# Graph network, two layers on one core: the products with the count matrix as whole float32 products, degrees in two halves, moments of x1 by accumulators

## What is computed

```python
h = relu(layernorm(x))
# layer 0
msg = (h[src] + edge) @ Wm.T + bm
agg = segment_sum(msg, dst) / max(deg, 1)
u   = concat(h, agg) @ Wu.T + bu
o   = layernorm(h + gelu(u)) * gamma + beta
x1  = x + o
# layer 1
h1    = relu(layernorm(x1))
neigh = segment_sum(h1[src], dst)
y     = relu(((1 + eps) * h1 + neigh) @ W1 + b1) @ W2 + b2
out   = x1 + y + h1
```

## Time and profile before

| | us |
|---|---|
| median of 3 runs | 487.54 (486.55 to 487.87) |
| the profiled execution | 488.46 |
| span of the profiled execution | 486.7 |
| TensorE busy (matmul) | 471.4 |
| VectorE busy | 266.0 |
| ScalarE busy | 165.5 |
| GpSimd busy | 120.6 |

### The profile page before, as it was taken

The page is one execution under the profiler, slowest core; times in us unless marked ns, Lnnn a source line. Parts: engine busy times, 40 slices in busy tenths (PEclk is TensorE's granted clock), DMA queues, the critical chain, the costliest instruction groups (busy, mean ns, idle before and its releaser), DMA issues.

```text
span 486.7 us, 9356 instructions
## 1 busy us (share of the span) xinstructions
PE 471.4 (97%) x3297; PEld 281.4 (58%) x3297; DVE 266.0 (55%) x614; ACT 165.5 (34%) x312; POOL 120.6 (25%) x185
## 2 busy tenths in 40 slices
PE   7999999999999999999999999899999999999997
PEld 5545545455545456777766655799744449444442
DVE  4798886778787878876958699923000000011011
ACT  6677642333333338412047287620012213000000
POOL 4016343443344331000001113249980000000000
PEclk9999999999999999989999999999999999999999
DMA  8999999999999999996330111040230000010111
GB/s 283 382 396 408 408 386 373 403 392 406 401 373 393 407 404 398 369 349 237 147 105 23 43 43 40 5 170 1 56 118 0 0 0 1 22 43 23 43 43 38
DMA packets 31720, 98.92 MB, mean 203 GB/s; under 512 B 3672, under 2 KB 4696, under 8 KB 31674
## 3 DMA queue, kind: packets, MB, share of 16 engines
q1 hardware_dynamic: 30458, 97.27, 52.9%
q10 hardware_dynamic: 1216, 1.05, 0.7%
HBM read 95.76 MB, written 2.56 MB: 202 GB/s over the span
## 4 chain that ended last, share of the span: by engine, by line
PE 82%; DVE 8%; issue 4%; DMA 2%; DVEq 1%; POOL 1%; ACT 1%; SPq 0%; POOLq 0%
PE ps L1452 14%; PE ps L1437 14%; PE ps L1170 11%; PE ps L1218 6%; PE ps L1189 6%; PE ps L1384 4%; PE ps L1198 4%; PE ps L1279 4%; PE ps L1360 3%; PE ps L1280 3%; PE ps L1361 3%; PE ps L1122 3%; PE ps L1178 2%; DMA WmN<-in_L_gnn_Wm_dram 1%; DVE acc L790 1%
## 5 line engine op out<-in xcount | busy, mean ns | idle before, releaser
L438 POOL TENSOR_TENSOR aggT<-turned_sums,aggT 128x88 f32 x118 | 61.0, 517 | 97.3 <-ACT turned_sums L511 84.3
L746 DVE TENSOR_TENSOR A<-ps,A 128x220 f32 x158 | 60.7, 384 | 33.1 <-PE ps L1189 24.2
L1088 DVE TENSOR_TENSOR U<-ps,U 128x512 f32<-128x512 f32 (+1 forms) x10 | 6.9, 692 | 128.5 <-PE ps L1452 128.5
L1452 PE MATMUL ps<-W2s,hid 128*128 128x512 f32 (+1 forms) x160 | 68.8, 592 | 0.0
L1437 PE MATMUL ps<-aggT,W1s 128*128 (+1 forms) x192 | 67.3, 513 | 0.0
L1170 PE MATMUL ps<-ea,oneD 128*22 128x256 f32 x944 | 62.6, 383 | 3.2 <-issue 2.2
L1437 PEld LDWEIGHTS ps<-aggT,W1s 128*128 128x128 f32 x192 | 36.4, 190 | 30.7 <-issue 30.6
L1170 PEld LDWEIGHTS ps<-ea,oneD 128*22 128x22 f32 x944 | 23.3, 101 | 50.1 <-issue 26.3
L1452 PEld LDWEIGHTS ps<-W2s,hid 128*128 128x128 f32 (+1 forms) x160 | 30.0, 188 | 38.2 <-issue 38.2
L505 ACT COPY packed_sums<-ps 128x256 f32<-128x256 f32 x59 | 22.0, 372 | 80.9 <-PE ps L1170 80.7
L1360 PE MATMUL ps<-AR,Hh 128*128 128x256 f32 (+2 forms) x160 | 44.0, 311 | 0.7 <-DVE Hl L1055 0.7
(11 more groups left out here) (149 smaller groups left out, 651.8 us busy)
## 6 DMA issues: line engine op xcount, KB each, us to landing
ea<-in_edge_attr_dram SPq DMA_DIRECT2D x78, 1024.0 KB, 8.7
X<-in_x_dram SPq DMA_DIRECT2D x1, 2304.0 KB
xt<-in_x_dram SPq DMA_DIRECT2D x9, 256.0 KB, 3.6
out_dram<-U SPq DMA_DIRECT2D x9, 256.0 KB
W1s<-in_L_gnn_W_dram SPq DMA_DIRECT2D x1, 2048.0 KB, 9.0
W2s<-in_L_gnn_W_dram SPq DMA_DIRECT2D x1, 2048.0 KB, 8.3
Wu2N<-in_L_gnn_Wu_dram ACTq DMA_DIRECT2D x2, 512.0 KB, 4.4
WmN<-in_L_gnn_Wm_dram SPq DMA_DIRECT2D x1, 1024.0 KB, 7.2
```

Of the source, the lines that this page charges most:

```text
L438: nc.gpsimd.tensor_tensor(cols, sums, cols, ALU.add).then_inc(early_step, 1)
L746: V.tensor_tensor(cols, ps[:, 4 + m % 2, half * KW:(half + 1) * KW].rearrange("p (h w) -> p h w", w=W), cols, ALU.add).then_inc(add_step, 1)
L1452: last = T.matmul(ps[0:rows, 6 + b % 2, :], hid[:, k, b * P:b * P + rows], W2s[:, k, :], start=k == 0, stop=k == KC - 1)
```

## The change

Each pair of products (Hh and Hl) becomes one product of `X` with the counts, both of type float32. `Hh` and `Hl` go, and with them the splitting on ScalarE and VectorE in both layers, as well as one of the three additions per tile on GpSimd. The path for large counts goes, with the maximum over `Dsum`, its transpose and the branches. The 10 degree products are split over two pairs of steps, and `BIAS_AT`, `HAS_AT` place the additions of the biases at other steps. The moments of x1 come from an accumulator in `add_x` and a square with an accumulator on ScalarE. ScalarE converts A further ahead (CONV_AHEAD), and the pieces behind the loop stand at other places. The last tile of y is computed, added and stored in two halves of 256 columns.

```diff
-    Hl, _ = place("Hl", [P, NT, D], F32R, x_at)
-    Hh, hh_at = place("Hh", [P, NT, D], F32R)
-    ARc, arc_at = place("ARc", [P, NT, 512], F32R)
-    AR, _ = place("AR", [P, NT, NP], F32R, stream_at)
+    ARc, arc_at = place("ARc", [P, NT, 512], F32)
+    AR, _ = place("AR", [P, NT, NP], F32, stream_at)
...
-    DEG_AT = FOLD_AT[-1] + 3
+    DEG_AT = FOLD_AT[-1] + 2
+    DEG_PARTS = [range(0, NT // 2), range(NT // 2, NT)]
-    BIAS_AT = [n for n in range(DEG_AT - 2, DEG_AT + NT - 1) if n != OUT_AT]
-    HAS_AT = [min(OUT_AT + 1 + b, NG - (NT - b + 1) // 2) for b in range(NT)]
+    BIAS_AT = [n for n in range(EARLY + 3, EARLY + NT + 4) if n != OUT_AT]
+    HAS_AT = [NG - (NT - b + 1) // 2 for b in range(NT)]
+    Y_HALVES = [slice(0, D // 2), slice(D // 2, D)]
+    Y_BANK = [6 + b % 2 for b in range(NT)] + [2]
+    CONV_AHEAD = 4
...
-                    pe.wait_ge(low0_ready, c + 1)
+                    pe.wait_ge(h0_ready, c + 1)
...
-                    T.matmul(to, Hh[:, c, rows], here, start=c == 0 and (q < 2 or f % 2 == 0), stop=False)
-                    last = T.matmul(to, Hl[:, c, rows], here, start=False, stop=c == NT - 1 and (q < 2 or f % 2 == 1))
+                    last = T.matmul(to, X[:, c, rows], here, start=c == 0 and (q < 2 or f % 2 == 0), stop=c == NT - 1 and (q < 2 or f % 2 == 1))
...
-                pe.wait_ge(split1, b + 1)
+                pe.wait_ge(h1_ready, b + 1)
...
-                    T.matmul(to, Hh[:, b, rows], AR[:, b, start:start + cols], start=b == 0 and (cols == 512 or f % 2 == 0), stop=False)
-                    last = T.matmul(to, Hl[:, b, rows], AR[:, b, start:start + cols], start=False, stop=b == NT - 1 and (cols == 512 or f % 2 == 1))
+                    last = T.matmul(to, X[:, b, rows], AR[:, b, start:start + cols], start=b == 0 and (cols == 512 or f % 2 == 0),
+                                    stop=b == NT - 1 and (cols == 512 or f % 2 == 1))
...
-                if DEG_AT - 1 in pair:
-                    degree_products()
+                for part, at_step in zip(DEG_PARTS, (DEG_AT, DEG_AT + 2)):
+                    if at_step in pair:
+                        degree_products(part)
...
-                late((0, 0, 2, 3, 3)[b])
+                late((0, 0, 3, 0, 4)[b])
...
-                    late(2)
+                    late(3)
...
-            def h1_high(b):
-                act.wait_ge(h1_ready, b + 1)
-                nc.scalar.copy(Hh[:, b, :], X[:, b, :]).then_inc(hi1_ready, 1)
+            def x1_squares(b):
+                act.wait_ge(x1_mean, b + 1)
+                act.wait_ge(piece_mm, 2 * NT + b + 1)
+                nc.scalar.activation(X[:, b, :], U[:, b, :], ACT.Square, bias=mv2[:, b, 0:1], accum_out=mv2[:, b, 1:2]).then_inc(x1_square, 1)
...
-            full_conv(1)
+            h0_again(1)
+            for c in range(1, CONV_AHEAD):
+                full_conv(c)
             for k in range(NT + 4):
-                if k + 2 < NT:
-                    full_conv(k + 2)
-                for work, lag in ((gelu, 0), (h1, 3), (h1_high, 3), (h1T, 3)):
+                for work, lag in ((gelu, 0), (h0_again, 0), (x1_squares, 2), (h1, 3), (h1T, 3)):
...
+                for c in range(CONV_AHEAD + 2 * k, min(CONV_AHEAD + 2 * k + 2, NT)):
+                    full_conv(c)
...
-                if n == FOLD_AT[-1] + 1:
-                    dve.wait_ge(fold_step, HB - 1)
-                    V.tensor_reduce(most[:], Dsum[:], AX.X, ALU.max).then_inc(fold_step, 1)
...
-                V.scalar_tensor_tensor(U[:, b, :], tt[b % TB][:], rs[:, b:b + 1], xt[b % TB][:], ALU.mult, ALU.add).then_inc(x1_ready, 1)
+                V.scalar_tensor_tensor(U[:, b, :], tt[b % TB][:], rs[:, b:b + 1], xt[b % TB][:], ALU.mult, ALU.add,
+                                       accum_out=x1_sum[:, b:b + 1]).then_inc(x1_ready, 1)
...
-                V.bn_stats(stats[:, b, :], U[:, b, :]).then_inc(x1_stats, 1)
-                V.bn_aggr(mv2[:, b, :], stats[:, b, :]).then_inc(x1_aggr, 1)
+                V.tensor_scalar(mv2[:, b, 0:1], x1_sum[:, b:b + 1], -1.0 / D, None, ALU.mult).then_inc(x1_mean, 1)
...
-                V.tensor_tensor(Hl[:, b, :], X[:, b, :], Hh[:, b, :].bitcast(F32), ALU.subtract).then_inc(split1, 1)
...
-                for k in range(KC):
-                    last = T.matmul(ps[0:rows, 6 + b % 2, :], hid[:, k, b * P:b * P + rows], W2s[:, k, :], start=k == 0, stop=k == KC - 1)
-                last.then_inc(y_mm, 1)
+                for half, cols in enumerate([slice(0, D)] if b < NT - 1 else Y_HALVES):
+                    for k in range(KC):
+                        last = T.matmul(ps[0:rows, Y_BANK[b + half], 0:cols.stop - cols.start], hid[:, k, b * P:b * P + rows], W2s[:, k, cols],
+                                        start=k == 0, stop=k == KC - 1)
+                    last.then_inc(y_mm, 1)
```

More of the change, by code:

```diff
@@ L23 @@
 EPS = 1e-5
-COUNT_MAX = 4096
 PREP_FIRSTS = 3
@@ L398, in _ @@
             sp.wait_ge(conv, NT)
-            sp.wait_ge(past_large, 1)
             sp.dma_start(W2s[:], W2.rearrange("(k p) d -> p k d", p=P)).then_inc(w2_in, 16)
-            for b in range(NT):
-                rows = P if b < NT - 1 else TAIL
+            for b in range(NT - 1):
                 sp.wait_ge(y_done, b + 1)
-                sp.dma_start(out[b * P:b * P + rows, :], U[0:rows, b, :]).then_inc(stored, 16)
-            sp.wait_ge(stored, 16 * NT)
+                sp.dma_start(out[b * P:(b + 1) * P, :], U[:, b, :]).then_inc(stored, 16)
+            for half, cols in enumerate(Y_HALVES):
+                sp.wait_ge(y_done, NT + half)
+                sp.dma_start(out[(NT - 1) * P:N, cols], U[0:TAIL, NT - 1, cols]).then_inc(stored, 16)
+            sp.wait_ge(stored, 16 * (NT + 1))
         @block.gpsimd
@@ L447, in _ @@
                     nc.gpsimd.tensor_tensor(rs0[:], ve[:], mhalf[:], ALU.pow).then_inc(rs_ready, 1)
-            for k in range(NT + 1):
+            for k in range(NT + 2):
+                if k >= 2:
+                    b = k - 2
+                    pool.wait_ge(ve2_ready, b + 1)
+                    nc.gpsimd.tensor_tensor(rs2[:, b:b + 1], ve2[:, b:b + 1], mhalf[:, 0:1], ALU.pow).then_inc(rs2_ready, 1)
                 if k < NT:
@@ L598, in _ @@
                 piece_conv(i)
-            act.wait_ge(most_ready, 2)
-            large = act.value_load(most1[0:1, 0:1], min_val=0, max_val=E + P)
             act.wait_ge(sum_step, 2 * (NG - EARLY))
             act.wait_ge(piece_mm, 2 * NT)
-            with act.If(large > COUNT_MAX):
-                for c in range(NT):
-                    ins = nc.scalar.copy(AR[:, c, :], A16[:, c, 0:NP])
-                ins.then_inc(extra_conv, 1)
-                act.wait_ge(extra_add, NX * NT)
             def full_conv(c):
@@ L894, in _ @@
                     bias_out()
-                for b in range(NT):
-                    if HH_AT[b] == n:
-                        low_h0(b)
                 for c in range(1, HB):
@@ L1080, in _ @@
             dve.wait_ge(rst_done, 4)
-            with dve.If(large > COUNT_MAX):
-                extra(1)
-            V.nop().then_inc(past_large, 1)
-            for b in range(NT):
+            for b in range(NT - 1):
                 dve.wait_ge(y_mm, b + 1)
-                dve.wait_ge(res_step, 3 * b + 3)
-                rows = P if b < NT - 1 else TAIL
-                V.tensor_tensor(U[0:rows, b, :], ps[0:rows, 6 + b % 2, :], U[0:rows, b, :], ALU.add).then_inc(y_done, 1)
+                dve.wait_ge(res_step, 2 * b + 2)
+                V.tensor_tensor(U[:, b, :], ps[:, 6 + b % 2, :], U[:, b, :], ALU.add).then_inc(y_done, 1)
+            dve.wait_ge(res_step, 2 * NT)
+            for half, cols in enumerate(Y_HALVES):
+                dve.wait_ge(y_mm, NT + half)
+                mine = U[0:TAIL, NT - 1, cols]
+                V.tensor_tensor(mine, ps[0:TAIL, Y_BANK[NT - 1 + half], 0:D // 2], mine, ALU.add).then_inc(y_done, 1)
         @block.tensor
@@ L1199, in turn, with degree_products @@
                 last.then_inc(turned, 1)
-            def degree_products():
-                pe.wait_ge(fold_step, HB)
-                T.transpose(ps[0:1, DEG_BANK, 256:256 + P], most[:], ident[:])
-                for d in range(NT):
+            def degree_products(part):
+                pe.wait_ge(fold_step, HB - 1)
+                for d in part:
                     last = T.matmul(ps[:, DEG_BANK, 384 + d:385 + d], Dsum[:, d * P:(d + 1) * P], onesF[:, 0:1], start=True, stop=True)
@@ L1424, in _ @@
             last.then_inc(rst_mm, 1)
-            with pe.If(large > COUNT_MAX):
-                pe.wait_ge(rst_done, 4)
-                extra(1)
             pe.wait_ge(w1_in, 16)
```

138 lines of the change are left out of this document (29 added, 109 removed).

## The result

The changed kernel takes **556.2 us** (555.62 to 556.57, 4 executions) against 487.71 of the kernel before in the same comparison: the ratio is 1.1408 (95% interval 1.1387 to 1.1430), 68.5 us slower. Forecast were 555.0 and +67.4. Its profiled execution took 556.39 with a span of 554.6, where the earlier trace rows belong to a span of 486.7.

What follows compares the result with a forecast made beforehand. TensorE, busy 97% of the span, was taken as the bound. 75.6 - 3.5 - 0.1 - 4.1 - 0.5 = +67.4 us on the profiled 488.46 gave 555.9, or a median of 555.0, range 549 to 561.

Steps and rivals of the forecast that it cites:

- The price of a product: Loop and behind it: whole float32 products at 0.8585 us instead of 0.467 per pair at 512 columns, +75.6 us in all.
- Waits (-1.4): In the loop, TensorE's waits on VectorE, including the one ahead of the first piece, shrink: -1.4 us, bounds 0 and -1.5.
- Clock (-1.0): In the loop after the degree products, halves reduce time lost at the lower clock: -1.0 us, bounds -1.7 and +1.7.
- Switches (-1.0): In the loop, switching between edge products and pieces gets cheaper between two float32 kinds: -1.0 us, bounds 0 and -2.
- part 2: What TensorE gets back in the loop from waits, clock, one transpose less and switches: -3.5 us.
- Bias places (0): In the loop, later bias additions cost nothing, VectorE having room from removed work and longer steps: 0 us.
- Behind the loop: After the loop, 44.1 us more product time, less 4.1 of TensorE's 5.2 us of waits absorbed.
- the first rival: Behind the loop, h1's chain with one more engine hop keeps TensorE waiting: 559 to 562 us, chance 0.10.
- the fourth rival: All products: four passes against two, so a whole product costs exactly two pairs: 571 us, chance 0.02.
- the clock falls more often: Rival, in the loop: each half of the degree products drops the clock, 557.7 to 560 us, chance 0.08.
- more comes back: Rival, whole kernel: all waits, seams and clock losses are recovered, 552 us or some 549, chance 0.07.
- products with the counts cost what pairs do: Rival, all products with the counts: no added product time, so 479 us, chance 0.02.

Runs made afterwards that it cites:

- Run 1: Kernel before with each pair replaced by one whole float32 product of Hh with the counts, Hl still computed but not multiplied: 558.74 us, ratio 1.1470.
- run 2: Changed kernel with each whole product replaced by two float32r products of the same h, no splitting, so neighbour sums come out doubled: 482.68 us, ratio 0.9905.
- run 6: Kernel before, pairs kept, with y's last tile and the degree products in halves and the bias additions at the changed kernel's steps: 488.54 us, ratio 1.0030.
- run 9: Kernel before, pairs kept, with y's last tile and the degree products in halves, bias additions at their old steps: 485.73 us, ratio 0.9963.
- experiment 3: Changed kernel with one float32r product in place of each whole one, the low part of h left out: 450.68 us, ratio 0.9248.
- run 4: Changed kernel with the ten degree products together again in one pair of steps, four executions: 556.30 us.
- run 11: Changed kernel with the ten degree products together again, repeated in six executions: 557.13 us.
- run 5: Kernel before with only y's last tile in two halves; pairs, splitting and degree products together as before: 486.97 us, ratio 0.9983.
- run 8: Kernel before with y in halves, x1's moments by accumulators and the new ScalarE order; pairs, bias places and degree products together as before: 485.98 us, ratio 0.9955.
- run 12: Changed kernel as it is, repeated in six executions: 556.20 us.
- run 10: Kernel before with all parts of the change except whole products and bias places; pairs, splitting and large-count path stay: 484.38 us, ratio 0.9929.
- run 7: Kernel before with every part of the change that needs no whole products, moved bias additions included; pairs and splitting stay: 487.41 us, ratio 1.0000.

## Why the prediction was right

- **The price of a product (+75.6).** Right in size and place. Measured were 0.8585 at 512 columns, and 0.43 and 0.38 at 256 and 226. The step that carried it was to take the distance of starts instead of durations: by the mean durations in the earlier trace rows the pair looks nearly as dear as the whole. Run 1 shows the price alone, +70.7; run 2 shows it from the other side, 73.5. Both are below 75.6: run 2 by the 2.2 us of waits that the longer products absorb, run 1 by the larger waits of the kernel before.
- **The loop.** Forecast 31.3 - 3.6 = 27.7 later at its end, measured 277.46 - 249.55 = 27.9. That these agree so closely is luck. The waits and the clock each gave about 0.5 us more than forecast, and the switches gave nothing of their 1.0.
  - *Waits (-1.4)*: -1.9 by TensorE's starts, 0.5 of it ahead of the first piece, where 0.18 remains. The other 1.4 are behind it. Before, the edge products of three pairs of steps took 2.25, 2.54 and 2.02 us, where 1.87 is usual and where all take 1.87 or 1.88 now, and 0.2 were lost right behind the first piece. The trace shows only 0.6 of this as idle time, ending on `oneD`.
  - *Clock (-1.0)*: -1.5 between the two profiled executions. The run of two pieces behind the degree products takes 5.45 us before (215.89 to 221.34), the others 3.93. The reasoning was incomplete: what I took for a property of the kernel happens in some executions and not in others, and halves make it rarer.
  - *Switches (-1.0)*: wrong, 0. A run of pieces carries 0.2 us for its switches with either form (7.07 - 6.87 now, 3.93 - 3.74 before).
  - *The transpose (-0.1)*: counted twice, once in the 3.5 of part 2 and once more in the sum. The trace shows none of it: transpose and degree products took 2.26 us before, and the two halves take 1.14 each.
  - *Bias places (0)*: right for the changed kernel, where no wait on `oneD` is left in the loop. Of the cover that I named, the removed work is enough (run 2). Without it and without longer steps the places cost 2.8 us (runs 6 and 9).
- **Behind the loop.** Forecast 44.1 - 4.1 = 40.0, measured 138.5 - 97.7 = 40.8. Only some 0.15 us of waits are left, and 0.3 in seams, less than the 1.1 that I kept. The waits lie where the prediction put them, between the first two transposes of h1. In order of time:

```profile
313.33 0.60 PE L1276 MATMUL ps<-ident,X 128*128 128x128 f32 x4
313.76 3.60 PE L1291 MATMUL ps<-CT,aggT 128*128 128x512 f32 x8
317.34 0.66 PE L1276 MATMUL ps<-ident,X 128*128 128x128 f32 x4
317.83 3.60 PE L1267 MATMUL ps<-AR,X 128*128 128x512 f32 x8
```

  The map takes 3.43 from 313.76 and the transposes start at 317.34, 0.15 later. What I missed is the transposes themselves, 0.43 per tile now (313.33 to 313.76) and 0.35 in the earlier trace rows, and some 0.4 of product time at 226 and 256 columns. VectorE's idle time there ends mostly on TensorE, as forecast, but 10.8 us of it end on ScalarE's square (below, in us, times, longest). It is the extra hop that the first rival feared, and TensorE's longer products hide it:

```profile
DVE ve L977 <- ACT X L593: 10.8, 7, 4.1
```

- **VectorE's accumulator**, which no row of before showed: its read takes 0.08 us, less than the 0.19 that I used.

```profile
L968 DVE DVE_READ_ACCUMULATOR U<-tt,rs,xt 128x1 f32 x10 | 0.8, 82 | 0.0
```

- **The end (-0.5).** Measured -0.84.
- **The whole.** The spans differ by 67.9 us: 27.9 in the loop, 40.8 behind it, -0.8 at the end. The medians differ by 68.5, since the profiled execution of the kernel before had a fall of the clock and lay above its median.
- **The rivals.** The h1 chain fell with runs 1 and 2. That the clock falls more often fell too: it is 1.000 in all ten executions of the changed kernel. That more comes back (552 or less) fell with the time itself. That products with the counts cost what pairs do fell with the rows above. The two-to-one ratio of the fourth rival did not come out: 0.8585 / 0.467 is 1.84. But experiment 3 shows why. A single float32r product takes 0.233, and at the granted 2.4 GHz 512 columns are 0.213, so that fits one pass and 0.02 besides. The whole product is 4 x 0.213 = 0.853 and 0.005 besides. At 256 and 226 columns it is four times the columns and 0.005 as well (0.432 and 0.382). The four passes of the Trainium skill ("FP8 and Floating Point Precision", TensorE Precision Notes) agree with these times, and it was the pair that cost more than two.

What stays open is why the clock falls in some executions only. Counted by the mean granted clock of each execution (a fall where it is 0.997 or less):

| degree products | runs | executions with a fall |
|---|---|---|
| together, whole products | 1, 4, 11 | 6 of 14 |
| together, pairs | 5, 8 | 16 of 24 |
| halves, whole products | changed kernel, 12 | 0 of 10 |
| halves, pairs | 2, 9, 10 | 0 of 22 |
| halves, pairs, subtraction and moved bias | 6, 7 | 6 of 24 |

So putting the products in halves does keep the clock up, but not where TensorE also waits for long: 3.4 us on `oneD` in runs 6 and 7, where runs 9 and 10 have 0.6 and 0.7. In run 6's profiled execution the fall came right behind the first half, and ahead of that half TensorE had waited 1.70 us for `oneD`:

```profile
215.09 1.07 PE L1187 MATMUL ps<-ea,oneD 128*22 128x128 f32 x32 [1.70 <-DVE oneD L720]
```

Run 3 has halves too, and in both of its executions the mean clock is 0.992; its fall lies between 270 and 300 us, where TensorE waited for h1. That waits and thin products add up is a reading of these cases and was not tested by itself.

## What to carry to other kernels

Price a product by the distance between the starts of successive ones, never by the mean of overlapping records, and multiply it out before weighing what other engines save. Two float32r products with a split of one operand cost TensorE 54% of one whole float32 product at 512 columns, so the split pays as long as the other engines have room for it. A schedule is tuned to the load around it: the same places of ten additions of 0.69 us are free in one version and cost 2.8 us in its neighbour. So parts of a change are to be judged one by one: here the parts that need no whole product were worth 3.6 us, once the bias places were left as they were. And one profiled execution can't tell whether a clock falls; the mean clocks of a dozen executions can.

## What the runs showed of the hardware

- A float32r product takes 0.233 us at 512 columns, 0.1134 at 256 and 0.112 at 226. At 2.4 GHz the columns alone are 0.213, 0.107 and 0.094, so what comes besides is not constant (0.020, 0.007, 0.018), and between 256 and 226 columns hardly anything is gained. A whole float32 product is four times its columns and 0.005 us at each of these widths: 0.8585, 0.432 and 0.382.
- A float32 product leaves two records of 592 ns at 512 columns, 0.8585 us apart per product, and a float32r product one of 390 to 400 ns, 0.233 apart. Their mean durations say nothing of their prices.
- The clock can fall with TensorE never idle, behind some 2.3 us of one-column products (run 11, busy for 12.00 of 12.00 us at a clock of 0.86). By chance it did so in 22 of 38 executions of the variants that have them together, in 0 of 32 with them in halves and without the 3.4 us of waits of runs 6 and 7. A fall costs 1.4 to 1.7 us, and a kernel's executions then lie in groups that far apart.
- Reading an accumulator takes 0.08 us on VectorE and 0.19 on ScalarE.
